# Flamingo layer on one core: the first scores of a batch issued between the third and fourth part of K

## The reference

```python
qh = heads_split(layernorm(x) @ Wq); kh = heads_split(ctx @ Wk); vh = heads_split(ctx @ Wv)
dots = jnp.einsum('bhid,bhjd->bhij', qh, kh) * scale
dots = jnp.where(mask[:, None, :, :], mask_value, dots)
attn = jax.nn.softmax(dots, axis=-1)
out = jnp.einsum('bhij,bhjd->bhid', attn, vh)
x = x + jnp.tanh(g_xattn[0]) * (merge_heads(out) @ Wo + bo)
...
xf = layernorm(x)
idx = jnp.argmax(softmax(xf @ Wg + bg), axis=-1)        # one expert for each row
y = gelu(xf @ W1[idx] + b1[idx]) @ W2[idx] + b2[idx]
x = x + jnp.tanh(g_ffn[0]) * y
```

## Time and profile before

| what | value |
|---|---|
| device time, median of 3 runs | 215.0 us (213.63, 215.0, 215.24) |
| the profiled execution, device time | 213.29 us |
| its span in the trace | 211.5 us |
| mean granted TensorE clock | 0.993 of full speed |
| PE busy | 196.0 us (93%) |
| PEld busy | 144.4 us (68%) |
| DVE busy | 126.3 us (60%) |
| ACT busy | 103.5 us (49%) |
| POOL busy | 89.3 us (42%) |

### The profile page before, as it was taken

How to read it: one execution, slowest core, us unless ns; L and a number is a source line. 1 busy time by engine, 2 the same in 40 slices (tenths; PEclk the granted TensorE clock), 3 DMA queues, 4 the chain that set the end, 5 groups by cost and what they waited for, 6 DMA issues and landing times.

```text
span 211.5 us, 4026 instructions
## 1 busy us (share of the span) xinstructions
PE 196.0 (93%) x1284; PEld 144.4 (68%) x1284; DVE 126.3 (60%) x525; ACT 103.5 (49%) x372; POOL 89.3 (42%) x129
## 2 busy tenths in 40 slices
PE   7899989889999999999999789998999999979950
PEld 7753477557767454688895656775788999859940
DVE  0589873799899232154327899989834347265520
ACT  1221532799999321302217699998541254435510
POOL 7000090557577940000000799776930003777460
PEclk9999999999999999999999999999999999999997
DMA  4994188999999200290000011600000000254010
GB/s 112 348 391 170 33 284 294 329 313 326 286 200 342 81 2 0 67 329 0 3 0 2 14 52 38 206 2 0 3 0 2 3 0 25 88 170 137 33 54 21
DMA packets 21185, 25.16 MB, mean 119 GB/s; under 512 B 1875, under 2 KB 19741, under 8 KB 21024
## 3 DMA queue, kind: packets, MB, share of 16 engines
q1 hardware_dynamic: 19136, 22.51, 35.0%
q0 software_dynamic: 1152, 2.12, 3.0%
q10 hardware_dynamic: 864, 0.15, 0.4%
HBM read 14.14 MB, written 11.68 MB: 122 GB/s over the span
## 4 chain that ended last, share of the span: by engine, by line
PE 61%; issue 14%; DVE 7%; DMA 6%; ACT 6%; POOL 3%; POOLq 0%; DVEq 0%; ACTq 0%
PE s_bank L1580 13%; PE o_bank L1663 7%; PE t_bank L1637 7%; PE o_bank L1537 7%; PE s_bank L1620 6%; PE s_bank L1689 4%; ACT probs L768 4%; PE o_bank L1656 4%; PE s_bank L1880 3%; DMA rows<-in_x_dram 3%; PE o_bank L1891 2%; DMA oT<-sorted_rows 2%; PE t_bank L1671 2%; DVE probs L1225 1%; DVE pT L1246 1%
## 5 line engine op out<-in xcount | busy, mean ns | idle before, releaser
L608 POOL TENSOR_TENSOR probs<-probs,r_col 128x512 f32<-128x512 f32 x32 | 33.4, 1043 | 62.1 <-DVE r_col L1236 61.7
L768 ACT ACTIVATE probs<-probs,negm_run 128x160 f32<-128x160 f32 x128 | 53.0, 416 | 5.2 <-DVE negm_run L1225 5.0
L1225 DVE CUSTOM_DVE_ANT_0 probs<-s_bank,maskneg 128x160 f32<-128x160 f32 x128 | 33.1, 318 | 5.8 <-PE s_bank L1620 5.5
L1580 PE MATMUL s_bank<-xnT,wq_sb 128*128 128x512 f32 x64 | 28.8, 598 | 0.3 <-ACT xnT L721 0.3
L1537 PE MATMUL o_bank<-wo_sb,oT 128*128 128x256 f32 x128 | 28.6, 379 | 0.0
L1537 PEld LDWEIGHTS o_bank<-wo_sb,oT 128*128 128x128 f32 x128 | 23.9, 190 | 3.5 <-issue 0.5
L768 ACT ACTIVATION_READ_ACCUMULATOR probs<-probs,negm_run 128x1 f32 x128 | 24.0, 187 | 0.0
L1620 PE MATMUL s_bank<-k_sb,q_sb 64*128 64x160 f32 x256 | 22.3, 311 | 0.0
L1620 PEld LDWEIGHTS s_bank<-k_sb,q_sb 64*128 64x128 f32 x256 | 17.9, 186 | 4.8 <-issue 4.0
L1580 PEld LDWEIGHTS s_bank<-xnT,wq_sb 128*128 128x128 f32 x64 | 11.7, 190 | 13.4 <-issue 13.3
L1637 PE MATMUL t_bank<-ident,probs 128*128 128x128 f32 x128 | 18.7, 284 | 1.7 <-issue 1.1
(11 more groups left out here) (150 smaller groups left out, 306.3 us busy)
## 6 DMA issues: line engine op xcount, KB each, us to landing
sorted_rows<-empty_row SPq DMA_DIRECT2D x8, 1040.0 KB, 14.1
oT<-in_L_ffn_W_dram SPq DMA_DIRECT2D x1, 2048.0 KB, 19.0
q_sb<-in_L_ffn_W_dram SPq DMA_DIRECT2D x1, 2048.0 KB, 8.4
oT<-sorted_rows SPq DMA_DIRECT2D x1, 1040.0 KB, 5.3
oT<-sorted_rows SPq DMA_DIRECT2D x8, 130.0 KB, 2.4
rows<-in_x_dram SPq DMA_DIRECT2D x2, 512.0 KB, 8.7
wq_sb<-in_L_xattn_Wq_dram SPq DMA_DIRECT2D x1, 1024.0 KB, 8.6
mask_sb<-in_mask_BxSxS_bk_dram SPq DMA_DIRECT2D x2, 512.0 KB, 10.6
```

The lines of the kernel that those rows point to most:

```text
L608: nc.gpsimd.tensor_tensor(window_wide(u), window_wide(u), r.rearrange("p i h -> p (i h)") .unsqueeze(2).broadcast_to([P, 4, WIDE]), ALU.mu ...
L768: last = nc.scalar.activation(window_part(u, i, h), window_part(u, i, h), ACT.Exp, bias=negm_run[at], scale=-1.0, accum_out=l_run[at])
L1225: nc.vector.tensor_tensor_reduce(window_part(u, i, h), s_bank[u % 2][:, h, i * CK:i * CK + WK], maskneg[:, q, 0:WK], -SCALE, LARGEST, ALU. ...
L1580: last = nc.tensor.matmul(bank[m % 4], wq_sb[:, c, m * P:(m + 1) * P], xnT[:, c, b * N:(b + 1) * N], start=(c == 0), stop=(c == DC - 1))
```

## The change

Part u of K goes to bank `u - 1`, so parts 1 and 2 lie in `s_bank[0]` and parts 3 and 4 in `s_bank[1]`. With that TensorE issues the scores of unit 0 after K's third part, as soon as parts 1 and 2 have been copied, and makes K's fourth part after them. VectorE takes the maxima of unit 0 between its two copies of K, in batch 1 ahead of the router's steps. ScalarE does the exponentials of unit 0 ahead of its copy of V. The wide transposes of the first job wait for one copy of V only (bank 4 must be free); the wait for the other copies stands ahead of the left transposes (bank 7).

```diff
         def window_k_dst(u):
-            return k_sb[:, 2 * u - 2:2 * u, 0:WK], bank[u % 4].rearrange("p (m k) -> p m k", m=2)[:, :, 0:WK]
+            return k_sb[:, 2 * u - 2:2 * u, 0:WK], bank[u - 1].rearrange("p (m k) -> p m k", m=2)[:, :, 0:WK]
...
+                window_exp(b, 0)
                 act.wait_ge(first.v_ps, b * 3 + 1)
                 nc.scalar.copy(*window_v_dst(0)).then_inc(first.v_act, 1)
-                for u in range(2):
-                    window_exp(b, u)
+                window_exp(b, 1)
                 act.wait_ge(first.v_ps, b * 3 + 3)
...
-                for u in range(1, KU, 2):
+                def take_k(u):
                     dve.wait_ge(first.k_ps, b * KU + (u + 1))
                     nc.vector.tensor_copy(*window_k_dst(u + 1)).then_inc(first.k_dve, 1)
+
+                take_k(1)
                 dve.wait_ge(first.mask_ready, b + 1)
+                window_max(b, 0)
+                take_k(3)
                 also("k")
-                for u in range(2):
-                    window_max(b, u)
+                window_max(b, 1)
                 also("v0")
...
                     if job >= 1:
 
                         pe.wait_ge(first.o_dve, b * JOBS + job)
+                    else:
+
+                        pe.wait_ge(first.v_act, b * 2 + 2)
+                        pe.wait_ge(first.v_dve, b * 2 + 2)
                     pe.wait_ge(first.pn_ready, 2 * (g + 2 * job + 2))
...
-                            last = nc.tensor.matmul(bank[u % 4][:, i * CK:i * CK + WK],
+                            last = nc.tensor.matmul(bank[u - 1][:, i * CK:i * CK + WK],
...
                     last.then_inc(first.k_ps, 1)
                     also(f"k{u}")
+                    if u == 3:
+
+                        pe.wait_ge(first.k_act, b * 2 + 1)
+                        pe.wait_ge(first.k_dve, b * 2 + 1)
+                        scores(0)
...
                 project_v(0)
                 pe.wait_ge(first.k_act, b * 2 + 2)
                 pe.wait_ge(first.k_dve, b * 2 + 2)
-                scores(0)
                 scores(1)
...
                     if job == 0:
-                        pe.wait_ge(first.v_act, b * 2 + 2)
-                        pe.wait_ge(first.v_dve, b * 2 + 2)
+
+                        pe.wait_ge(first.v_act, b * 2 + 1)
```

## The result

| what | before | after |
|---|---|---|
| device time, median of 20 runs each | 214.3 us (213.63 to 215.51) | 213.21 us (212.53 to 214.52) |
| ratio to before, 95% interval | | 0.9945 [0.9928, 0.9963], or 1.2 us less (0.8 to 1.5) |
| the profiled execution, device time | 213.29 us | 213.06 us |
| its span | 211.5 us | 211.3 us |
| mean granted TensorE clock | 0.993 | 0.992 |

In it the runs of either kernel stand in two groups by their mean granted clock, up to 0.985 (medians 214.99 us before, 214.48 after) and from 0.987 (213.81 and 213.24), so a median also moves with how many runs of each group it holds; inside the groups the change gives 0.51 and 0.57 us.

A forecast was written before the change was run, and what follows sets the result against it. TensorE, busy 34.99 of 35.00 us, bounds the steady attention, so only its earlier start in each batch gains. 0.65 (batch 0) + 0.6 (batch 1) = 1.25 us off the median 215.0 gives 213.75 us, range 211.7 to 215.1.

The forecast's parts named there:

- Batch 1, 0.6: Batch 1's opening: unit 2's maxima start 0.6 us earlier, between 0.1 and 0.75, mostly through the router's additions on VectorE.
- Held to 116.7: Batch 1: VectorE's router addition, ready at 116.43, waits for GpSimd until 116.7 and not 117.21, 0.5 us gained.
- Batch 0, 0.65: Batch 0's opening: unit 2's maxima start at 40.83 and not 41.47, 0.64, say 0.65 us gained, at most 0.95.
- This new wait costs 0.2 us: Batch 0: unit 0's moved scores wait on TensorE for the copy of K's part 2, 0.2 us.
- I take 0.1 for a change back: TensorE in the openings: each return from products over 64 rows to 128 costs 0.1 us.
- The exponentials: Batch 0, ScalarE: unit 1's exponentials end by 39.6, before the left keys' V is there at 39.90.
- (1): Rival: VectorE's router steps stay slow in batch 1, which gains 0.1; in all 0.75 less, 214.25 us; chance 0.20.
- (2): Rival: 128/64-row changes expose the 0.76 us weight load in each opening; in all 0.2 slower, 215.2 us; chance 0.09.
- (3): Rival: something later, such as loads or scatters, does not move with TensorE; time stays 215.0 us; chance 0.11.
- (4): Rival: openings give 0.95 + 0.75 and the steady part improves; over 2.1 us less, 212.8 or less; chance 0.07.
- One sign that the prediction named as against it: Stages behind the openings: the prediction is wrong if they take another time than before; no size given.

The follow-up runs named there:

- e4: The kernel before with GpSimd's bias addition moved behind the multiplications of batch 0; ratio to before 1.0003 [0.9977, 1.0030].
- e10: The kernel before with one more GpSimd pass over the bias ahead of its bias addition; ratio to before 0.9998 [0.9974, 1.0022].
- e12: A copy of the kernel before, nothing changed; ratio to before 1.0017 [0.9996, 1.0037].
- e5: The changed kernel measured again, nothing edited; ratio to before 0.9965 [0.9938, 0.9991], 0.75 us less.
- e1: The changed kernel with the new order in batch 0 only, the new K banks in both batches; ratio to before 0.9988 [0.9962, 1.0015].
- e8: The kernel before with the router's four place steps ahead of unit 0's sum on VectorE in batch 1; ratio to before 1.0002 [0.9974, 1.0029].
- e2: The changed kernel with the new order in batch 1 only, the new K banks in both batches; ratio to before 0.9986 [0.9960, 1.0012].
- e6: The changed kernel with VectorE's copy of K's part 2 ahead of the mask step in batch 0; ratio to before 0.9934 [0.9906, 0.9963].
- e7: The changed kernel with the router's four place steps ahead of unit 0's sum on VectorE in batch 1; ratio to before 0.9952 [0.9927, 0.9978].
- e11: The changed kernel with the edits of e6 and e7 together; ratio to before 0.9941 [0.9915, 0.9967].

## Why the prediction was right, and where it was not

**The number.** Forecast 1.25 us less, measured 1.2 (0.8 to 1.5) and 0.75 (0.2 to 1.3). The path in the table, which leaves out the landing of the first loads and the last writes, was 172.34 to 172.73 in four executions with both openings old and the router in its place (before, e4, e10, e12), and 171.91 and 171.38 after: 0.4 to 1.35 less. That 1.25 lies near the measured times is in part luck: 0.65 of it was to come from batch 0, which by the marks gave -0.22 (after), 0.35 (e5) and 0.08 (e1). The time forecast, 213.75, lies 0.5 over the measured 213.21, since the kernel before came to 215.0 in three runs and to 214.3 in twenty. Two slips in the sums weigh nothing: 213.29 - 1.25 is 212.04, and the range's lower end takes off 1.6 where the upper gains add up to 0.95 + 0.75 = 1.7.

**Batch 1, 0.6: right, by its mechanism.** The sum of unit 0 came 0.90 earlier, GpSimd's multiplication with it, and the additions fell to 0.18 and 0.19. "Held to 116.7" was not seen: V's copy came no earlier (the forecast had 0.1), and at 117.14 the addition met no hold any more (GpSimd's second multiplication ends at 116.80 + 0.40 = 117.20), so the two errors cancel. e8 shows the same without the change. The rule that the prediction cited from the Trainium skill, SBUF — State Buffer, section Who interferes with whom, agrees with 0.68 beside GpSimd and 0.19 without.

**Batch 0, 0.65: wrong, in two steps.** "This new wait costs 0.2 us": in three executions of the changed kernel or its batch 0 half (after, e5, e1) the delay was 0.72, 0.15 and 0.42. The 0.2 was worked out from rows of one execution, and for that one it held, 31.77 + 0.75 + 0.14 - 29.10 - 3.43 = 0.13; by the same sum from e12, e8 and e2, which all run batch 0 in the old order, it would have been 0.6 to 0.8. I read when the copy ended and did not ask what it stood behind: a mask step of 3.42 us that takes 0.49 elsewhere. "I take 0.1 for a change back": it was 0.41 in batch 0 (e6), half of it from the scores and half from K's parts, which take longer apart than together, and 10.04 - 9.85 = 0.19 in batch 1, where K's parts stood apart already and the scores alone take longer. Without any delay batch 0 gains 0.50, and not 0.65 + 0.2.

**The exponentials** no longer end last, as forecast, and the table load stands right behind the copy of K's part 3 (109.47), off the path.

**The rivals.** (1) fell: the router's addition took 0.18 or 0.19 in every execution of the new batch 1. (2) had the right place and too high a price: the switch costs 0.2 to 0.4 in an opening, not 0.76 more, and decides nothing. (3) fell for the change, whose middle kept its length and whose last stage was no longer than before's, but it is what happened to the places in e7, e8 and e11. (4) did not occur.

**What stays open.** By the marks the change is worth 0.60 plus 0.50 less the delay, with delays of 0.15 to 0.72, so 0.4 to 0.95 us; the first measurement, 1.2, is above that though its interval reaches into it. One sign that the prediction named as against it, another time of the stages behind the openings, did show: 78.86 and not 79.29. The last stage is a candidate for the rest: it took 79.29 in one of the four old orders and 78.9 in the others, 78.9 in all five with the whole change and the router in its place, and 79.3 in both with half of the change (e1, e2). That is too few executions to say that the change brings it about, and the kernel before alone shows both. In all of these the second router's first scatter begins 55.02 to 55.03 us after batch 1's first values, and VectorE's step that waits for the experts' rows 65.8 to 65.95 after them in the three long ones and 65.55 to 65.7 in the others. So the difference arises between the scatter and the landing of its rows; what sets it there was not tried.

## What to carry to other kernels

A wait that has microseconds of cover in the old order may have none in the new one: before work is moved ahead, each thing that it will wait for is followed back one step more, to what stands ahead of it on its engine, and an instruction that takes several times as long as its twin elsewhere is asked what holds it. A margin of 0.2 us between two chains that hang on different loads is not a number, since it moves by half a microsecond from one execution to the next. And a gain at a mark is worth nothing until the last stage has been read too: of two gains of 0.5 us in the openings, that of K's copy stayed and that of the places was taken back.

## What the hardware showed beyond that

VectorE's mask step, which writes 128 x 640 bf16 in SBUF, takes 0.49 us alone and 3.4 to 4.8 beside GpSimd's addition, ending 0.34 to 0.35 after it; a copy out of PSUM ran in 0.49 beside the same addition (e6). The Trainium skill, SBUF — State Buffer, section Who interferes with whom, says that a two-port VectorE operation and GpSimd exclude each other for a whole instruction; the rows of the mask step agree, though no row shows that this step is such an operation.

Score products of 64 rows, eight in a row of the trace, take 0.74 to 0.75 us by themselves and 1.29 for sixteen together.

GpSimd's addition started and K's first product started 1.2 to 1.9 us apart in executions of the same order of work, since each hangs on another load, as e5 shows (29.10 - 27.25 = 1.85 in before, 29.47 - 28.20 = 1.27 in after, 30.14 - 28.30 = 1.84 in e5, 29.53 - 28.36 = 1.17 in e2).
